# Macaron block on one core: POOL normalises in the first feed-forward, and four turned tiles go through DMA transposes of 16-bit halves

## The reference

```python
x = x + 0.5 * ffn(layernorm(x))
x = x + attention(layernorm(x))      # the attention normalises a second time, then scales by ln_w, ln_b
x = x + 0.5 * ffn(layernorm(x))
# ffn: 8 experts, all of them computed: h = gelu(xf @ w1[e] + b1[e]); y = sum over e of (h @ w2[e] + b2[e])
#      times norm_g, the gate's top probability g made g / (g + 1e-6); gate logits go through an RMS norm and a softmax
# attention: 8 heads of 8, q and k brought to unit length, causal softmax(8 q.k), output projection
```

## Time and profile before

| | before |
|---|---|
| median of three runs | 269.75 us (269.66 to 269.92) |
| the profiled execution | 269.82 us, its span 268.1 us |
| first feed-forward | about 6 to 108 us |
| attention | about 103 to 180 us |
| second feed-forward | from about 180 us |

### The profile page before, as it was taken

The page is one execution under the profiler, slowest core; times in us unless marked ns, Lnnn a source line. Parts: engine busy times, 40 slices in busy tenths (PEclk is TensorE's granted clock), DMA queues, the critical chain, the costliest instruction groups (busy, mean ns, idle before and its releaser), DMA issues.

```text
span 268.1 us, 5428 instructions
## 1 busy us (share of the span) xinstructions
PE 258.2 (96%) x1829; PEld 183.6 (69%) x1829; DVE 216.2 (81%) x590; ACT 217.5 (81%) x344; POOL 80.7 (30%) x175
## 2 busy tenths in 40 slices
PE   7999999999999999979998999999999999999995
PEld 6886878888788786533434433378888887888783
DVE  7999899998898987797378587378889678697784
ACT  2897668859878889999999999987777867859673
POOL 6302104204850482664349545520200000200100
PEclk9999999999999999999999999999999999999999
DMA  5741200001012104101314003300004211210311
GB/s 152 219 123 23 58 1 2 0 1 39 2 34 46 42 2 78 40 1 22 62 39 82 2 4 78 80 1 4 0 8 111 42 39 39 39 34 9 80 39 39
DMA packets 33343, 11.51 MB, mean 43 GB/s; under 512 B 24130, under 2 KB 32548, under 8 KB 33316
## 3 DMA queue, kind: packets, MB, share of 16 engines
q1 hardware_dynamic: 33172, 11.11, 17.7%
q10 hardware_dynamic: 144, 0.07, 0.1%
HBM read 4.88 MB, written 2.62 MB: 28 GB/s over the span
## 4 chain that ended last, share of the span: by engine, by line
PE 73%; DVE 8%; ACT 7%; issue 5%; POOL 4%; DMA 2%; SPq 0%; POOLq 0%; DVEq 0%; ACTq 0%
PE ps L590 10%; PE ps L596 10%; PE ps L608 10%; PE ps L593 10%; PE ps L613 10%; PE ps L611 9%; PE ps L746 5%; ACT probs L937 3%; PE ps L708 2%; PE ps L777 2%; ACT h L924 2%; POOL probs L1533 1%; POOL w_raw L1527 1%; DMA kT<-k_stack 1%; DVE h_lo L1100 1%
## 5 line engine op out<-in xcount | busy, mean ns | idle before, releaser
L924 ACT ACTIVATE h<-ps,cols 128x512 f32<-128x512 f32 x128 | 88.0, 694 | 36.2 <-PE ps L596 32.6
L1100 DVE TENSOR_TENSOR h_lo<-h,h_hi 128x512 fp32r<-128x512 f32 x128 | 88.6, 698 | 19.1 <-ACT h_hi L927 16.7
L937 ACT ACTIVATE probs<-ps 128x1024 f32<-128x1024 f32 (+1 forms) x80 | 65.0, 918 | 1.5 <-PE ps L708 1.4
L590 PE MATMUL ps<-xT_hi,w_hi 128*128 128x512 f32 x128 | 51.5, 402 | 0.0
L608 PE MATMUL ps<-h_hi,w_hi 128*128 128x512 f32 x128 | 50.5, 395 | 0.3 <-ACT yT L949 0.3
L927 ACT ACTIVATE h_hi<-ps,cols 128x512 fp32r<-128x512 f32 x73 | 50.2, 688 | 0.0
L613 PE MATMUL ps<-h_lo,w_hi 128*128 128x512 f32 x128 | 50.2, 392 | 0.0
L596 PE MATMUL ps<-xT_lo,w_hi 128*128 128x512 f32 x128 | 49.9, 390 | 0.0
L593 PE MATMUL ps<-xT_hi,w_lo 128*128 128x512 f32 x128 | 49.9, 390 | 0.0
L611 PE MATMUL ps<-h_hi,w_lo 128*128 128x512 f32 x128 | 49.9, 389 | 0.0
L746 PE MATMUL ps<-probs,v_ones 128*32 128x512 f32 (+4 forms) x384 | 34.2, 458 | 0.9 <-POOL probs L1533 0.6
(11 more groups left out here) (141 smaller groups left out, 273.2 us busy)
## 6 DMA issues: line engine op xcount, KB each, us to landing
w_raw<-in_L_ffn_w SPq DMA_DIRECT2D x8, 256.0 KB, 4.6
turned<-blocks SPq DMA_DIRECT2D x6, 256.0 KB, 2.0
w_raw<-turned SPq DMA_DIRECT2D x24, 64.0 KB, 2.3
w_raw<-v_ones SPq DMA_DIRECT2D x8, 128.0 KB, 2.4
x_sb<-in_L_attn_x SPq DMA_DIRECT2D x3, 256.0 KB, 6.8
out_x<-x_sb SPq DMA_DIRECT2D x3, 256.0 KB, 2.3
w_raw<-o_scaled SPq DMA_DIRECT2D x2, 256.0 KB, 4.3
x_sb<-in_L_attn_x SPq DMA_DIRECT2D x2, 128.0 KB, 2.3
```

Source lines behind the costliest of these rows:

```text
L590: pe.matmul(bank, w1_hi[:, w], xT_hi[:, cols_g], start=True, stop=False)
L924: first = nc.scalar.activation(h[:, slot, :], ps[:, BANK_H + slot, :], ACT.Gelu, bias=bias)
L937: nc.scalar.activation(probs[:, s % P_SLOTS, :, 0:width], ps[:, bank:bank + 2, 0:width], ACT.Exp, scale=SCALE).then_inc(exp_done, 1)
L1100: dve.tensor_tensor(h_lo[:, slot, :], h[:, slot, :], h_hi[:, slot, :].bitcast(f32), ALU.subtract).then_inc(split_done, 1)
```

## The change

POOL takes over `normalise` in the first layer for groups 1 to 3 and for the attention norms of groups 0 to 2. Four turned tiles no longer go through PE: y of group 0, the attention norm of group 0, and the features of groups 2 and 3. POOL copies the float32 words of such a tile (512 a partition) into two planes of 16-bit halves (`make_planes`), SP issues one DMA transpose of the 128x1024 halves (`turn_planes`), and POOL joins the turned halves to words again (`join_planes`), in `landed` or straight in `xf`. DVE adds y of group 0 from `landed`, and ACT's `affine_features(0)` reads it from there. The statistics of group 2 move to the end of group 0; the qkv products of group 0 and its squares, sums and guesses move from the turn of groups 1 and 2 into group 2; the gate product of group 2 goes to chunk 0; the high parts of group 0 go to group 3's chunk 0, those of group 1 from its chunk 8 to 10. In POOL's queue the order is written out anew.

```diff
-AT_ONE = dict(AT, gate_product=0)
-AT_THIRD = dict(AT, ln_normalise=(2, 3), ln_transpose=5, ln_copy=5, ln_low=7,
-                att_normalise=(10, 11), qk_high=9, gate_product=5, gate_logits=6, gate_shift=12, gate_tanh=13, gate_weight=14)
+AT_ONE = dict(AT, gate_product=0, residual=(6, 7), att_stats=(8, 9), att_aggregate=10)
+AT_THIRD = dict(AT, ln_copy=8, ln_low=9, gate_product=0, gate_logits=1, gate_shift=12,
+                first_affine=3, first_qkv=5, qk_squares=6, qk_copy=7, qk_sums=7, qk_guesses=8, gate_tanh=13, gate_weight=14)
...
+            def turn_planes(n):
+                sp.wait_ge(planes_done, n + 1)
+                sp.dma_start_transpose(planes_t[:, :, :].rearrange("p w (t q) -> p (w t) q", q=P),
+                                       planes[:, :, :].rearrange("p w c -> p (w c)")).then_inc(planes_in[n], 16)
+
+            turn_planes(0)
+            sp.wait_ge(joined, 1)
+            turn_planes(1)
+            sp.wait_ge(xf_done[FFN], PLANED_FFN[0] + 1)
+            turn_planes(2)
+            sp.wait_ge(joined, 2)
+            turn_planes(3)
...
-                    if second and c in at["next_stats"]:
+                    if F < 2 and c in at["next_stats"]:
                         dve.wait_ge(x_in[g + 2], 16)
                         stats(FFN, g + 2, halves[at["next_stats"].index(c)])
...
+            def normalise(kind, n, g):
+
+                pool.wait_ge(rstd_done[kind], n + 1)
+                for i in range(GROUP_TILES):
+                    pool.tensor_scalar(xn[:, kind, i, :], x_sb[:, GROUP_TILES * g + i, :], mean_var[:, kind, i, 0:1],
+                                       rstd[:, kind, i:i + 1], ALU.subtract, ALU.mult).then_inc(xn_done[kind], 1)
+
+            def by_plane(words):
+                return words.bitcast(u16).rearrange("p (c w) -> p w c", w=2)
...
+            def make_planes(words):
+                pool.tensor_copy(planes[:, :, :], by_plane(words)).then_inc(planes_done, 1)
+
+            def join_planes(n, words):
+                pool.wait_ge(planes_in[n], 16)
+                return pool.tensor_copy(by_plane(words), planes_t[:, :, :])
...
+                if layer == 0 and g == 0:
+                    ln_once(1)
+                    pool.wait_ge(ln_t[FFN], 1)
+                    normalise(FFN, 1, 1)
+                    gate_root(0)
+                if layer == 0 and g == 1:
+                    pool.wait_ge(y_evac, PLANED_Y + 1)
+                    make_planes(yT[:, :])
+                    ln_once(2)
+                    pool.wait_ge(ln_t[FFN], 2)
+                    normalise(FFN, 2, 2)
+                    pool.wait_ge(xn_done[FFN], GROUP_TILES * 3)
+                    pool.wait_ge(planes_in[0], 16)
+                    make_planes(token_rows(FFN))
+                    join_planes(0, landed[:, :]).then_inc(joined, 1)
+                    gate_root(1)
+                    pool.wait_ge(gate_mm, 2)
+                    pool.wait_ge(xT_ready, 2)
+                    join_planes(1, xf[:, FFN, :]).then_inc(xf_done[FFN], 1)
+                    ln_twice(0)
+                    normalise(ATT, 0, 0)
+                    pool.wait_ge(xn_done[ATT], GROUP_TILES)
+                    make_planes(token_rows(ATT))
+                    ln_once(3)
+                    normalise(FFN, 3, 3)
+                if layer == 0 and g == 2:
+                    pool.wait_ge(xn_done[FFN], GROUP_TILES * 4)
+                    pool.wait_ge(planes_in[2], 16)
+                    make_planes(token_rows(FFN))
+                    pool.wait_ge(resid, GROUP_TILES)
+                    join_planes(2, landed[:, :]).then_inc(joined, 1)
+                    gate_root(2)
+                    pool.wait_ge(gate_mm, 3)
+                    pool.wait_ge(xT_ready, 3)
+                    join_planes(3, xf[:, FFN, :]).then_inc(xf_done[FFN], 1)
+                    ln_twice(1)
+                    pool.wait_ge(planes_done, 3)
+                    normalise(ATT, 1, 1)
+                    inverse_lengths(pool, 0)
+                    unit_vectors(pool, 0)
+                if layer == 0 and last:
+                    low_parts(pool, 0)
+                    inverse_lengths(pool, 1)
+                    ln_twice(2)
+                    pool.wait_ge(ln_t[ATT], 1)
+                    normalise(ATT, 2, 2)
+                    unit_vectors(pool, 1)
+                    gate_root(3)
+                    low_parts(pool, 1)
```

More of the change, by code:

```diff
@@ L189, in build @@
         blocks = sb("blocks", [P, GROUP])
+        u16 = mybir.dt.uint16
+        planes = sb("planes", [P, 2, GROUP], u16)
+        planes_t = sb("planes_t", [P, 2, GROUP], u16)
+        landed = sb("landed", [P, GROUP])
         turned_dram = [nc.dram_tensor(f"turned{n}", (P, GROUP), f32, kind="Internal").ap() for n in range(TURNS)]
@@ L232, in build @@
         o_zero = sem("o_zero")
+        planes_done, joined = sem("planes_done"), sem("joined")
+        planes_in = [sem(f"planes_in{n}") for n in range(4)]
         job_filled, job_emptied = sem("job_filled"), sem("job_emptied")
@@ L643, in ffn_group @@
                         down(layer, F, 0)
-                        if operands and not first:
-                            y_transposes(F - 1, ln_groups=F + 1, att_groups=g - 1)
+                        if operands and g > 1:
+                            y_transposes(F - 1, ln_groups=2, att_groups=2 if last else 0)
                     if layer == 1 and first and c == 3:
@@ L648, in ffn_group @@
                     if c == at["gate_product"] and gate_product_of(layer, g) is not None:
-                        if operands and g >= 2:
+                        if operands and last:
                             pe.wait_ge(qkv_copied, g - 1)
@@ L669, in ffn_group @@
                         scores(1 + c - at["att_qkv"])
-                    if operands and 1 <= g < LAST and c == at["att_qkv"]:
+                    if operands and g == 2 and c == at["att_qkv"]:
                         qkv_products(g - 1)
@@ L876, in affine_features @@
             def affine_features(p):
-                act.wait_ge(ln_t[ATT], p + 1)
-                act.wait_ge(qkv_mm, p)
-                nc.scalar.activation(xf[:, ATT, :], ps[:, BANK_LN, :], ACT.Identity, bias=cols[:, COL_LNB:COL_LNB + 1],
+                if p == PLANED_ATT:
+                    act.wait_ge(joined, 2)
+                    normed = landed[:, :]
+                else:
+                    act.wait_ge(ln_t[ATT], p)
+                    act.wait_ge(qkv_mm, p)
+                    normed = ps[:, BANK_LN, :]
+                nc.scalar.activation(xf[:, ATT, :], normed, ACT.Identity, bias=cols[:, COL_LNB:COL_LNB + 1],
                                      scale=cols[:, COL_LNW:COL_LNW + 1]).then_inc(xf_done[ATT], 1)
@@ L978, in ffn_group @@
                             copy_qkv(g - 2)
-                        if c == at["qk_high"]:
-                            high_stacks(g - 2)
-                    if operands and 1 <= g < LAST and c == at["att_copy"]:
+                        if last and c == at["first_high"]:
+                            high_stacks(0)
+                        if last and c == at["qk_high"]:
+                            high_stacks(1)
+                    if operands and g == 2 and c == at["first_affine"]:
+                        affine_features(PLANED_ATT)
+                    if operands and g == 2 and c == at["att_copy"]:
                         affine_features(g - 1)
@@ L1133, in residual @@
                     xi = x_tile(g, i)
-                    y = y_rows(F) if landed else ps[:, bank, :]
+                    y = y_rows(F) if by_blocks else landed if F == PLANED_Y else ps[:, bank, :]
                     dve.scalar_tensor_tensor(xi, y[:, P * i:P * i + P], gate_half[:, F % 2, i:i + 1], xi,
@@ L1190, in ffn_group @@
                 at = schedule(layer, g)
-                second, third = (F == i for i in (1, 2))
-                made = F + 1 if F < LAST else 2 * GROUPS - 1 if F == GROUPS else None
+                made = {0: 1, GROUPS: 2 * GROUPS - 1}.get(F)
                 for c in range(CHUNKS):
-                    if c == at["ln_aggregate"] and made and not third:
+                    if c == at["ln_aggregate"] and made:
                         wait_stats(FFN, made)
@@ L1219, in ffn_group @@
                             aggregate(FFN)
-                    if made:
+                    if layer == 1 and made:
                         for half in range(2):
@@ L1237, in ffn_group @@
                             aggregate(ATT)
-                        for half in range(2):
-                            if c == at["att_normalise"][half]:
-                                normalise(ATT, g - 1, g - 1, halves[half])
                     if operands and g >= 2:
@@ L1479, in ffn_group @@
                     ln_once(2 * GROUPS - 1)
-                if third:
-                    low_parts(pool, g - 2)
-                if layer == 0 and g == 1:
-                    ln_twice(g - 1)
```

(1 more changed line is left out.)

65 lines of the change are left out of this document (35 added, 30 removed).

## The result

| | before | after |
|---|---|---|
| median of the runs | 269.77 us (269.66 to 269.92, 4 runs) | 288.0 us (287.21 to 289.3, 4 runs) |
| span of the profiled execution | 268.1 us | 286.2 us |
| mean granted clock of TensorE | 0.998 | 0.964 |

The ratio is 1.0682, with an interval of 1.0662 to 1.0701: 6.8% slower. The forecast was 268.9, its range ended at 271.6, and the dearest rival at 273.

A forecast was written before the change was run, and what follows sets the result against it. PE, busy 96% of a 268.1 us span, was taken as the bound, with DVE next. Terms -1.8 - 0.2 + 0.4 + 0.7 = -0.9 us took 269.82 to 268.9 us; range 267.6 to 271.6.

The forecast's parts named there:

- the dearest rival: POOL copies hold DVE off, above all in group 1; with 2.2 us copies 272 to 273 us; chance 0.19.
- What left PE: Four sets of four transposes leave PE's queue in the first feed-forward and attention norm: 1.8 us off.
- Start, -0.2: POOL normalises group 1 at 312 ns per operation, ready before PE asks at about 24.6: 0.2 us off.
- End of group 0, +0.4: Second pair of group 2's statistics stands ahead of gate_shift on DVE, delaying tanh, y and PE: 0.4 us added.
- Plane copies at 1.2 us, DMA transposes at 3.3: Groups 1 and 2: copy, transpose and copy back arrive in time, covered by ACT's three-chunk lead: 0.
- Unit vectors, +0.7: Group 3: POOL's norm work delays group 1's unit vectors, ACT's high parts and the exp table load: 0.7 us added.
- Shared access, 0: Group 1: long POOL operations hold DVE off, but its lead of two to three chunks takes that up: 0.
- DVE becomes the bound: Rival: each POOL copy holds DVE off, above all in group 1; 2.6 us more gives 271.5; chance 0.19.

The follow-up runs named there:

- the last version: Kernel after with all six normalisations on DVE, later affine step and qkv products, earlier group 2 statistics, gate product and group 3 normalisation at former chunks: 274.4 us, ratio 1.0166.

## Why the prediction was wrong

**What left PE: right in the count.** PE has 16 instructions fewer. No run measured the 1.8 us alone, and not all of it arrived: group 1 has lost three sets of four, 1.3 us by the earlier trace rows, and is 0.5 us shorter: 0.6 went into a wait for a cast of DVE that the kernel before did not have.

**Start, -0.2: wrong, and the largest error.** The failed step is the price "The nearest POOL row of that size is 312 ns". That row is of another operation, a select with a pattern; the same size and the same single input made it look near. The normalisation took 1.18 us in the mean and 1.37 here. The prediction's own bound from above, a loss of 0.3 at 0.8 us each, was too low as well. What it did to the chain was right: POOL has no slack there and PE asks at 24.6. With 5.47 us for the four, the same working gives a wait of 3 us, and 3.04 is what came. The clock behind it was not in the sum at all: 1.5 us in the median with a wait of 3.05 in the kernel before, 2.7 in the kernel after, where it was low for 5.4 us of PE's work.

**End of group 0, +0.4: right in the wait.** PE waits 0.69 us for y in place of 0.3, and the statistics moved forward take that away again. That the time follows is not shown: the stage's end moves by 0.6 us between runs with the same group 0.

**Plane copies at 1.2 us, DMA transposes at 3.3: right in the single price** (1.04 to 1.42 into planes; 1.3 to 1.9 back, a little over; 3.1 from issue to landing), **wrong in the conclusion.** "It is on time by one to two microseconds" held four normalisations for 1.3 to 2 us; they took 3.96, behind another four of 4.38. ACT's lead, the cover that was named, was used up, and PE waited 3.94 us.

**Unit vectors, +0.7: right mechanism, size off.** The four normalisations ahead of them were to take 1.3 to 2.1 us and took 3.75; the table load is 3.9 us later, reckoned from the evacuation in group 2. The step missed what follows, too: PE's wait of 2.1 us and the ten microseconds at half the clock, which go with the 2.7 us behind the table load. With all normalisations on DVE this stage is at 20.18 against 20.12 us of before.

**Shared access, 0: wrong.** The step "its lead of two to three chunks takes up the rest" counted a copy's length against DVE's total. The runs showed three things it missed. A chain of short operations loses a whole copy at each step, and has no lead of chunks. DVE's splits had no lead left: at the full clock, in the last version, PE still waits for them in group 2. And eight copies with nothing else cost 4.2 us at the full clock, 6.2 with the fall that their wait brought, so 0.5 to 0.8 each. The best version with planes adds 4.6 us at the full clock; with the 1.8 us that left PE (estimated, not measured) that makes 6.4, of which the copies alone account for 4.2. The other 2 us are not explained. The rival *DVE becomes the bound* had the mechanism, with a fifth of the chance. Its price, 2.6 us, is about half of the 5.5 that stay with the normalisations on DVE. What spoke against it was also counted too high: "DVE sheds 4 us in the same stretch" is 3.1 by the prediction's own numbers (23.95 less 20.8).

**Open.** Of the 2.7 us behind the table load, 2.1 go with the normalisations, and the lower clock goes with them; no run filled that wait. No run had the new order of the pieces without planes, so the 2 us named above can lie there. How the 6 us in group 2 divide between POOL's lateness and DVE's blocking cannot be summed: when the one is taken away, the other fills its place (31.16 and 30.58 us).

## What to carry to other kernels

An operation's price on POOL is looked up by its own form, with its scalars, and not by a neighbour of the same size; where no row shows it, four times the nearest row belongs inside the range. Taking a set of transposes from PE (0.44 us) by way of two POOL copies (0.5 to 0.8 us each through DVE) does not pay with DVE as full as here, 23.95 of 25.3 us. A stall of PE of some 3 us is to be booked with a range for the clock behind it: here 0 to 3 us on top of a wait of 3.05. Where the stall can't be avoided, useless products that end with it cover it. When runs of one kernel scatter, lay the mean granted clock of each beside its time before comparing medians.

## What the runs showed of the hardware

- A POOL operation with two scalars from SBUF has a fixed price of about 0.9 us (0.94 for 32 columns, 1.07 for 128, 2.44 for 512); with immediates 0.69 for 128. The select with a pattern takes 0.31 for 128.
- Two wide two-input operations with broadcast scalars (1.11 and 1.22 us in the kernel) do the work of four of these (3.75 to 5.79).
- A POOL copy of 128 x 1024 16-bit words takes 1.04 to 1.9 us, and a two-input DVE operation of 0.19 us takes up to 1.17 beside it, a cast of 0.42 up to 1.26; a reduction keeps its 0.19.
- After PE had stood for 3.05 us, its granted clock was at the lower level until about 31.7 us, 4.1 us from its first transpose (in the kernel after, behind 3.04 us, until 33.6); kept busy over the same stretch, it stayed at 1.0.
- The same stall is not always followed by the lower clock. With the stall of 3.05 us in the profile, the four runs had mean clocks of 1.0, 0.991, 0.991 and 0.986 and took 272.46, 274.06, 274.05 and 275.43 us. Behind the same wait of 2.3 us it fell in two profiles and stayed full in a third. Behind one of 2.07 us it was at 0.50 for ten microseconds in the kernel after.
